# Constant products at the joints, VectorE's chains laid between each other, rank products between key and value groups, in a four-stage transformer kernel

## What is computed

```python
x = x + jnp.tanh(g_xattn[0]) * _L0_xattn_ref(_layernorm(x), ctx, ctx, ...)      # 16 heads, softmax
x = x + jnp.tanh(g_ffn[0]) * _L0_ffn_ref(_layernorm(x), gamma, beta, Wg, ...)   # 8 experts, best 2
x = x + jnp.tanh(g_xattn[1]) * _L1_xattn_ref(_layernorm(x), ctx, ctx, fside, ...)  # with a bias
x = x + jnp.tanh(g_ffn[1]) * _L1_ffn_ref(_layernorm(x), slot_query, ...)        # 16 slots, one expert each
```

## Time and profile before

| | |
|---|---|
| runs | 1320.09, 1323.98, 1328.4 us; median 1323.98 |
| the profiled execution | 1323.91 us, span 1322.1 us, mean granted clock 0.985 |
| TensorE busy | 1268.1 us (96% of the span) |
| VectorE, ScalarE, GpSimd busy | 913.2, 796.0, 747.8 us |
| stages on TensorE | first attention to about 323 us, first expert stage to 775, second attention to about 1110, then the slots |

### The profile page before, as it was taken

How to read it: one execution, slowest core, us unless ns; L and a number is a source line. 1 busy time by engine, 2 the same in 40 slices (tenths; PEclk the granted TensorE clock), 3 DMA queues, 4 the chain that set the end, 5 groups by cost and what they waited for, 6 DMA issues and landing times.

```text
span 1322.1 us, 38089 instructions
## 1 busy us (share of the span) xinstructions
PE 1268.1 (96%) x14700; PEld 1136.9 (86%) x14700; DVE 913.2 (69%) x2362; ACT 796.0 (60%) x1739; POOL 747.8 (57%) x835
## 2 busy tenths in 40 slices
PE   7999999996999999999999988999999999999797
PEld 6888988885999999999999977899999998655476
DVE  4899999995766655566655037999999997321387
ACT  4667777663767777777775435666666655322454
POOL 1478888764577777877875044566666653100231
PEclk8999999998999999999999979999999999999999
DMA  6575555552777777777776610631111110699812
GB/s 214 189 250 200 174 200 194 166 200 66 258 219 222 219 227 238 216 224 217 226 238 241 278 49 26 241 117 50 50 50 50 50 46 22 253 428 426 322 59 71
DMA packets 103890, 237.50 MB, mean 180 GB/s; under 512 B 8992, under 2 KB 86176, under 8 KB 91296
## 3 DMA queue, kind: packets, MB, share of 16 engines
q1 hardware_dynamic: 97568, 218.29, 48.3%
q0 software_dynamic: 6144, 16.79, 3.9%
HBM read 174.22 MB, written 60.82 MB: 178 GB/s over the span
## 4 chain that ended last, share of the span: by engine, by line
PE 88%; DVE 6%; DMA 2%; issue 2%; ACT 1%; SPq 0%; POOL 0%; DVEq 0%; ACTq 0%; PEldq 0%; POOLq 0%
PE ps L2061 14%; PE psT L2046 7%; PE ps L690 6%; PE psS L667 5%; PE ps L1038 5%; PE ps L984 4%; PE psT L676 4%; PE psS L2046 3%; PE ps L2046 3%; PE ps L967 2%; PE ps L1001 2%; PE ps L911 2%; PE psT L682 2%; PE ps L701 2%; DMA arena<-wset_dram 2%
## 5 line engine op out<-in xcount | busy, mean ns | idle before, releaser
L2014 POOL TENSOR_TENSOR wb_lo<-arena,wb_hi 128x2048 fp32r<-128x2048 f32 x64 | 297.8, 4654 | 93.7 <-ACT wb_hi L2134 93.7
L2061 PE MATMUL ps<-wb_hi,hT_hi 128*128 128x256 f32 x528 | 151.6, 287 | 0.8 <-DVE hT_lo L2187 0.8
L676 PE MATMUL psT<-arena 32*128 32x128 f32 x2048 | 151.8, 287 | 0.4 <-ACT arena L1208 0.4
L2061 PE MATMUL ps<-wb_lo,hT_hi 128*128 128x256 f32 x528 | 147.7, 280 | 0.0
L2061 PE MATMUL ps<-wb_hi,hT_lo 128*128 128x256 f32 x528 | 147.6, 280 | 0.0
L667 PE MATMUL psS<-arena 32*128 32x256 f32 x1024 | 143.2, 398 | 0.7 <-ACT arena L1284 0.4
L2134 ACT CAST wb_hi<-arena 128x1024 fp32r<-128x1024 f32 x128 | 130.7, 1045 | 1.4 <-DMA arena<-w_dram 0.9
L676 PEld LDWEIGHTS psT<-arena 32*128 32x128 f32 x2048 | 126.9, 189 | 1.4 <-issue 0.9
L1623 POOL TENSOR_TENSOR arena<-arena,eps_sb 128x1 f32<-128x1 f32 x94 | 23.4, 249 | 156.2 <-DVE arena L1497 106.1
L2199 DVE TENSOR_TENSOR arena<-ps,arena 128x512 f32<-128x512 f32 (+1 forms) x39 | 25.4, 650 | 120.8 <-PE ps L2061 80.4
L1636 POOL DMA_INDIRECT arena<-xs_rows,slot_i x64 | 64.5, 1008 | 70.1 <-DMA xs_rows<-arena 55.1
(11 more groups left out here) (494 smaller groups left out, 3867.1 us busy)
## 6 DMA issues: line engine op xcount, KB each, us to landing
arena<-wset_dram SPq DMA_DIRECT2D x24, 2048.0 KB, 16.9
xs_rows<-arena SPq DMA_DIRECT2D x33, 1024.0 KB, 7.6
arena<-w_dram SPq DMA_DIRECT2D x32, 1028.0 KB, 5.8
arena<-w_dram SPq DMA_DIRECT2D x32, 1024.0 KB, 5.9
arena<-w_dram SPq DMA_DIRECT2D x7, 2052.0 KB, 13.6
w_sb<-xs_rows SPq DMA_DIRECT2D x33, 256.0 KB, 2.7
xs_rows<-arena SPq DMA_DIRECT2D x33, 256.0 KB, 5.5
arena<-ctxT_dram SPq DMA_DIRECT2D x63, 128.0 KB, 4.2
```

Source lines behind the costliest of these rows:

```text
L676: nc.tensor.matmul(psT[:, b, j * P:(j + 1) * P], kbd_[p, (k - 1) % NK, c, par, :], qT[p, (k - 1) % 3, c, :], start=j == 0, stop=False, ski ...
L2014: nc.gpsimd.tensor_tensor(wb_lo[:, u % 2, part], wb_raw[:, u % 2, part], wb_hi[:, u % 2, part], ALU.subtract).then_inc(w_g.sem, 1)
L2061: last = nc.tensor.matmul(ps[5][:, t * D:(t + 1) * D], hp[:, f, t * P:(t + 1) * P], wp[:, f, :], start=f == 0 and t == 0 and n == 0, stop= ...
```

## The change

It has four parts; the arithmetic on the data stays the same.

*The ends of the stages.* The first tables move from `setup` into step -1 of VectorE's loop, those made from columns alone stand in step -1, the rest behind the m chain of step 0 and without the wait for all constants. `keys(0)` goes to bank 2 and waits for its own load only; `values(0)` and the gate sums stand in step -1 behind the turned input; in steps 0 and 1 `values(k+1)` stands behind the second scores. The load of x[2] stands in setup, ahead of the wide output weights. ScalarE's copies of the first keys and values follow.

*Constant products.* Products of constants whose result nobody reads: 10 of 128 columns ahead of `keys(0)`, 14 of 512 columns at the end of the first attention, 5 behind the first `turned(0)` of the first expert stage, 8 ahead of the second attention's loop and 8 in its step 0 ahead of the row maxima.

*VectorE's order in the first attention.* The one-hot stands ahead of the statistics; the moments of tile k+2 between the reciprocal and `att`; the positions ahead of the moments' aggregate; the rows sent and normalised between the products and the sums of the slots; the logits, best values and best experts between the four pieces of the m chain (for the last steps at their old place).

*The ranks.* The two products stand between the two half groups of keys or values (steps 4 to 30); in steps 31 to 33 they stay, and those of tile 31 move from step 35 to step 34, between `ahead_keys(3)` and `ahead_values(3)`.

Counts of the semaphores are renumbered to fit. The diff, cut to its core:

```diff
+        def first_tables(dve):
+            dve.wait_ge(ld_first, 48)
+            nc.vector.tensor_scalar(qcol[:, 0, :], col["bq0"], QSCALE, None, ALU.mult)
+            nc.vector.tensor_tensor(bkm[:, :, :], col["bk0"][:, :, None].to_broadcast([P, C, 2]),
+                                    cv["parity"][:, None, :].to_broadcast([P, C, 2]), ALU.mult).then_inc(setup_v, 1)
+            for c in range(C):
+                last = nc.vector.tensor_scalar(wc[:, c, :], wg_sb[:, c, :], col["gamma"][:, c:c + 1], None, ALU.mult)
+            last.then_inc(fold_v, 1)
...
+            nc.vector.tensor_copy(ident_b[:, :], cv["ident"])
+            for j in range(4):
+                last = nc.vector.tensor_scalar(pick[:, j, :], ones[:, :], cv["pick"][:, j:j + 1], None, ALU.mult)
+            last.then_inc(setup_v, 1)
...
+        def column_tables(dve):
...
         def tables(dve):
-            dve.wait_ge(ld_const, 16 * 5)
...
-                    if A and valid(k + 4) and k + 4 >= 2:
+                    if A and valid(k + 4) and k + 4 >= 3:
...
                         if m:
+                            if i >= 5:
+                                ranks(i - 5)
                             pe.wait_ge(pre_a.sem, pre_a.at(i, "xT"))
...
                         if n_:
+                            ranks(i - 4)
                             pe.wait_ge(pre_a.sem, pre_a.at(i + 1, "xT"))
...
+                def ranks(i):
+                    pe.wait_ge(rk_v.sem, rk_v.at(i, "both"))
+                    before(pe, av_a.sem, av_a.at(i + 2, "av"))
+                    for n_, m in enumerate((before_r[:, :], both_rows[:, :])):
+                        last = nc.tensor.matmul(ps[4][:, n_ * E0:(n_ + 1) * E0], m, both[:, :], start=True, stop=True)
+                    last.then_inc(rk_p.sem, 1)
...
                 if A:
-                    gate_sums(pe)
-                    pe.wait_ge(ld_first, 48)
+                    pe.wait_ge(setup_v, 2)
+                    for _ in range(10):
+                        nc.tensor.matmul(ps[4][:, 0:P], ones[:, :], ones[:, :], start=True, stop=True)
                     pe.wait_ge(ld_kv, 16)
-                    keys(0, 6)
-                    values(0, 7)
+                    keys(0, 2)
                 else:
...
+                    for _ in range(8):
+                        nc.tensor.matmul(ps[4][:, :], ident_b[:, :], ident_b[:, None, :].to_broadcast([P, 4, P]),
+                                         start=True, stop=True)
...
+                    if A and k == -1:
+                        pe.wait_ge(ld_first, 48)
                     if A and valid(k + 1):
                         input_turned(k + 1)
+                    if A and k == -1:
+                        values(0, 7)
+                        gate_sums(pe)
...
-                        if A:
+                        if A and k == 2:
                             pe.wait_ge(pre_a.sem, pre_a.at(k + 1, "xT"))
-                        values(k + 1, 5 if A else 6)
+                        if not A or k == 2:
+                            values(k + 1, 5 if A else 6)
...
-                    if A and valid(k - 4):
-                        pe.wait_ge(rk_v.sem, rk_v.at(k - 4, "both"))
-                        before(pe, av_a.sem, av_a.at(k - 2, "av"))
-                        for n_, m in enumerate((before_r[:, :], both_rows[:, :])):
-                            last = nc.tensor.matmul(ps[4][:, n_ * E0:(n_ + 1) * E0], m, both[:, :], start=True, stop=True)
-                        last.then_inc(rk_p.sem, 1)
+                    if A and B - 2 < k < B + 3:
+                        ranks(k - 4)
...
                     scores(k, 1)
+                    if A and 0 <= k < 2:
+                        pe.wait_ge(pre_a.sem, pre_a.at(k + 1, "xT"))
+                        values(k + 1, 5)
...
+                    if not A and k == 0:
+                        for _ in range(8):
+                            nc.tensor.matmul(ps[4][:, :], ident_b[:, :], ident_b[:, None, :].to_broadcast([P, 4, P]),
+                                             start=True, stop=True)
                     if valid(k):
...
                         ahead_keys(3)
+                        ranks(B - 1)
                         ahead_values(3)
...
+                        pe.wait_ge(stash_a, 1)
+                        for _ in range(14):
+                            nc.tensor.matmul(ps[5][:, :], ident_b[:, :], ident_b[:, None, :].to_broadcast([P, 4, P]),
+                                             start=True, stop=True)
...
+                    if A and k == -1:
+                        act.wait_ge(setup_v, 3)
+                        act.wait_ge(kv_p.sem, key_at(0))
+                        keys(0, 2)
...
+                    if A and k == -1:
+                        act.wait_ge(kv_p.sem, value_at(0))
+                        values(0, 7)
...
+                def next_moments(dve, i):
+                    dve.wait_ge(ld_x[i % 2], dma_at(i, i % 2))
+                    nc.vector.bn_stats(stat[:, 0, :], x_all[:, i + 1]).then_inc(ln_v.sem, 1)
+
+                def logits(i):
+                    dve.wait_ge(out_v.sem, out_v.at(i, "t"))
+                    nc.vector.scalar_tensor_tensor(out=lg, in0=lg_sum, scalar=rq[:, 1:2], in1=bg_sb[:, :],
+                                                   op0=ALU.mult, op1=ALU.add).then_inc(rt_v.sem, 1)
+
+                def best_values(i):
+                    dve.wait_ge(rt_v.sem, rt_v.at(i, "lg"))
+                    nc.vector.max(top_val[:, i, :], lg).then_inc(rt_v.sem, 1)
+
+                def best_experts(i):
+                    dve.wait_ge(rt_v.sem, rt_v.at(i, "top"))
+                    nc.vector.max_index(idx8[:, :], top_val[:, i, :], lg).then_inc(rt_v.sem, 1)
...
+                        first_tables(dve)
...
-                    if A and k == 0:
-                        tables(dve)
...
-                    if A and valid(ln_i):
-                        dve.wait_ge(out_v.sem, out_v.at(ln_i, "x"))
-                        nc.vector.bn_stats(stat[:, 1, :], x_all[:, ln_i + 1]).then_inc(n2_v.sem, 1)
                     if A and valid(sl_i):
                         dve.wait_ge(rt_v.sem, rt_v.at(sl_i, "idx"))
                         nc.vector.tensor_tensor(oh2, idx8[:, 0:2, None].to_broadcast([P, 2, E0]),
                                                 cv["iota8"][:, None, :].to_broadcast([P, 2, E0]), ALU.is_equal)\
                             .then_inc(rk_v.sem, 1)
+                    if A and valid(ln_i):
+                        dve.wait_ge(out_v.sem, out_v.at(ln_i, "x"))
+                        nc.vector.bn_stats(stat[:, 1, :], x_all[:, ln_i + 1]).then_inc(n2_v.sem, 1)
+                    if A and valid(sl_i):
                         dve.wait_ge(rk_v.sem, rk_v.at(sl_i, "oh"))
                         before(dve, rk_p.sem, rk_p.at(sl_i - 1, "rank"))
                         nc.vector.tensor_tensor(both[:, :], oh2[:, 0, :], oh2[:, 1, :], ALU.add).then_inc(rk_v.sem, 1)
...
+                    if A and k == B + 3:
+                        normalised_rows(B - 1)
...
+                    if A and valid(nxt):
+                        next_moments(dve, nxt)
...
-                    if A:
-                        rows_sent(ln_i - 3)
-                    if A and k <= B:
-                        normalised_rows(ln_i)
...
                     if A and valid(sl_i):
                         dve.wait_ge(rk_p.sem, rk_p.at(sl_i, "rank"))
                         nc.vector.tensor_tensor(pos2, ps[4][:, 0:E0], next_row[:, :], ALU.add).then_inc(rk_v.sem, 1)
                         nc.vector.tensor_tensor(next_row[:, :], ps[4][:, E0:2 * E0], next_row[:, :], ALU.add)\
                             .then_inc(rk_v.sem, 1)
+                    if valid(nxt):
+                        dve.wait_ge(ln_v.sem, ln_v.at(nxt, "stats"))
+                        nc.vector.bn_aggr(mv[:, 0, :], stat[:, 0, :]).then_inc(ln_v.sem, 1)
+                    if A and k == -1:
+                        column_tables(dve)
                     if A and valid(sl_i):
                         dve.wait_ge(rk_v.sem, rk_v.at(sl_i, "run"))
                         nc.vector.tensor_tensor(ohp2, oh2, pos2[:, None, :].to_broadcast([P, 2, E0]), ALU.mult)\
                             .then_inc(rk_v.sem, 1)
+                    if A:
+                        rows_sent(ln_i - 3)
+                    if A and k <= B:
+                        normalised_rows(ln_i)
...
                         nc.vector.tensor_copy(m2[:, :, 0, :], mx).then_inc(mx_v.sem, 1)
+                        if A and valid(rt_i):
+                            logits(rt_i)
                         dve.wait_ge(mx_v.sem, mx_v.at(k, "hi"))
                         nc.vector.tensor_tensor(mrest, mx, m2[:, :, 0, :], ALU.subtract).then_inc(mx_v.sem, 1)
+                        if A and valid(rt_i):
+                            best_values(rt_i)
                         dve.wait_ge(mx_v.sem, mx_v.at(k, "rest"))
```

(30 more changed lines are left out.)

52 lines of the change are left out of this document (21 added, 31 removed).

## The result

| | before | after |
|---|---|---|
| median | 1326.10 us (11 runs) | 1312.34 us (11 runs, 1306.65 to 1325.62) |
| ratio | | 0.9911, 95% interval 0.9885 to 0.9937 |
| the profiled execution | 1323.91 us, span 1322.1, clock 0.985 | 1309.47 us, span 1307.7, clock 0.999 |

The ratio is -11.8 us, with its interval -8.3 to -15.2; the two profiled executions are 14.4 us apart. The forecast was 1308 with 1302 to 1318 as its range: right in sign and in most places; in size the median came out 4 us short. One place was not in the prediction at all, and it decides part of the spread of the changed kernel. One execution of the repetition x10, 1327.85 us, is more than 1.5% above the shortest of its kernel and is left out of its ratio.

What follows compares the result with a forecast made beforehand. PE was taken to bound the long stages, leaving gains at joints: start -6.4, VectorE's order 0, ranks +0.3, first attention's end -5.5, second attention's start -4.0; -15.6 from 1323.91 gives 1308.3 us, range 1302 to 1318.

Steps and rivals of the forecast that it cites:

- What bounds the kernel: Long middle stages: PE is the bound, so faster other engines cannot shorten the first attention's step; time is lost at joints.
- the ranks' move: First attention, two rank products moved into the middle of the group: -1 to +2.4 us over 27 steps, taken +0.3.
- Whatever a joint gives is handed on whole: All joints: gains pass on in full because the stages behind are PE-bound; the sum is made joint by joint.
- rival 5: Joints: the next wait, an expert weight's split or scatter's landing, takes the gains; each keeps a quarter, 1320 us; chance 0.04.
- The start: Kernel start: earlier keys and scores, shorter waits for m, and an avoided clock fall give -6.4 us, ends -2.5 and -7.5.
- rival 1: Early first attention: the clock falls again, start gives only -3.5, in all -12.7 us, 1311; chance 0.24.
- VectorE's order: First attention, some 28 steps: reordered instructions gain 0 because PE never waits for VectorE; ends 0 and +8.7 us.
- The end of the first attention: Joint to the first expert stage: earlier last scatter and full clock give -5.5 us together, ends -1.5 and -6.
- The second attention's start: Second attention's first steps: constant products keep the clock up, -4.0 us, ends -1.5 and -6.
- VectorE as the bound: First attention: VectorE, not PE, sets the step, so 8 to 13 us more come off, about 1297; chance 0.05.
- the late m chain: First attention, m of every step: the chain comes late and PE stalls, 1317 to 1330 us; chance 0.06.
- Further falls of the clock (1 and 2): Early first attention (1311 us, chance 0.24), or a later joint, first expert stage or second attention (about 1313, chance 0.15).

Runs made afterwards that it cites:

- x10: The unmodified changed kernel measured once more, beside others on the same chip: 1317.17 us, ratio 0.9911.
- x8: The changed kernel without the ten constant products at the very start: 1315.95 us, ratio 0.9894.
- x1: The changed kernel without any of its constant products, the rest of the change kept: 1319.92 us, ratio 0.9953.
- x6: The changed kernel with VectorE's plan of the six single units moved to the first expert stage's very start: 1308.40 us, ratio 0.9849.
- x7: x6 with the constant products of the second attention's start spread over its gaps (two, two, four, six): 1309.79 us, ratio 0.9842.
- x11: Repetition of x6, the changed kernel with the early plan of the single units: 1309.65 us, ratio 0.9864.
- x5: The changed kernel without the eight constant products ahead of the second attention's first row maxima: 1318.07 us, ratio 0.9915.
- x3: The kernel before with only VectorE's new order in the first attention and the ranks between the half groups: 1325.14 us, ratio 0.9978.
- x2: The kernel before with the constant products alone, at the same places: 1325.74 us, ratio 0.9990.
- x4: The kernel before with only the last tile's ranks moved, to between its keys and values made ahead: 1324.38 us, ratio 0.9989.
- x9: The kernel before with only VectorE's plan of the single units moved to the first expert stage's start: 1323.14 us, ratio 0.9957.

## Why the prediction was right, step by step

- *What bounds the kernel* held: no wait of PE in the first attention's middle, 8.80 us a step before and after, and, but for one stop of 1.3 us (see the ranks' move), all of the difference at joints. "Whatever a joint gives is handed on whole" did not hold in one place, the third unit of the first expert stage: of 4.9 us gained from m(31) to the second turn 1.95 were taken back in this execution, and 5.3 more in x8's. This is rival 5 in a form that was not in it: the text named a weight's split as what PE waits for, and it was GpSimd's split of the weights that held VectorE's plan. The kernel before shows its smaller form, 0.8 us, in the stretch that was read as bound by PE (432.16 of 433.00 us).
- *The start*: -6.4 forecast, -8.2 measured to m(3). Keys at 5.54 (5.1 forecast): they wait for the first context and not for their weights, since without the ten products they begin at 5.43 and 5.55 (x1, x8), released by that load. So the ten cost nothing there, as said, but their price was wrong: 4.37 us instead of 2.6, as each is listed as two products. First scores -4.7 against -2.4, outside its end of -3.5: mis-sized was the clock, up at 5.3 us instead of "a microsecond or two earlier" than 12.7, so queries and values ran at full clock too. The waits for m did not vanish as said (-1.1): PE then waited 0.46 and 0.76 us for ScalarE's copy of the queries. The fall from 22.9 to 29.8 us was avoided here and in x6, x7 and x11, which start alike. In x5 the clock fell from 18.6 to 25.4 us and m(3) came 3.4 us later than here, and in x10 it fell at 54.8; so rival 1 happened in part of the executions, and that the profiled one kept its clock is luck.
- *VectorE's order*: 0, measured 0 (x3). The m chain, whose serial end was priced +8.7, came no later than the product with m needed it.
- *The ranks' move*: +0.3; from m(4) to m(31) the change is -0.15 us over 27 steps. The other 1.3 us of that stretch is one stop of PE inside a group, with no semaphore behind it:

```profile
50.50 0.27 PE L695 MATMUL psT<-mT,pick 32*128 32x128 bf16 x3
51.95 0.32 PE L695 MATMUL psT<-mT,pick 32*128 32x128 bf16 x5 [1.18 <-issue]
```

  Stops in the same group, of 1.1 to 1.4 us, are in the profiles of x5, x7, x10 and x11 too, and shorter ones of about 0.3 us in x6 and x2. All seven kernels have the ten products at the start; the six without them (before, x1, x3, x4, x8, x9) have no such stop. That PE comes to this place earlier is not what separates them: in x5 it comes at 53.9 us and stops, in x1 at 53.5 and in x8 at 54.0 and does not. A load of instructions, 16 KB on a DMA queue of its own, begins 0.1 to 1.9 us ahead of the place in all thirteen profiles, so this alone is no reason either. The cause stays open; if the ten bring the stop, they give back 1 to 1.5 of the 3 us that they gain up to m(3).

- *The end of the first attention*: the scatter -2.9 (-2.6 forecast), of which the rows' load lost 0.7, since it came 2.5 us after the last scatter's end instead of 1.7; clock and turn -2.75 (-2.9 forecast). -4.9 in all against -5.5.
- *The second attention's start*: -3.5 against -4.0, in x10 -1.9; from the first turn to step 2 19.42 us, where 18.8 were forecast. That the second eight run while VectorE's chain is still going holds at full clock (x6); here the clock fell for 3.4 us.
- *Rivals.* VectorE as the bound and the late m chain fell (x3). Further falls of the clock (1 and 2) came in part of the executions; with the held instructions they are what the runs offer for a median of -11.8 where the forecast said -15.6: x6, which has none held there, has a ratio of 0.9849, 20 us under the kernel before.
- *The size.* -11.8 us lies nearer to rivals 1 and 2 (-12.7, and -11 to -13) than to the forecast, whose own range of 1304 to 1312 the median just misses. Being more than 1% faster was given 0.53 and being within 1% 0.44; it was 0.9%. Errors also offset each other in the profiled execution: the start gave 1.8 us more than its term, and the middle and the third unit, priced at 0.3 and at nothing, took 1.2 and 1.95.

## What to carry to other kernels

Look first for the stretches that run at half clock and for what PE waits for ahead of them: filling a wait at a joint with constant products was worth some 3 us there, as long as they end inside the wait; at half clock they can stick out. At the start the same products brought nothing with the old order around them, in the one profile of it. A chain on an engine that the bound never waits for can be shortened by an eighth and bring nothing. Where a gain is made ahead of a stage, look at the small waits inside that stage: 0.8 us before was the mark of a collision that grew to 6 in some profiles.

## What the runs showed of the hardware

Small instructions of VectorE, reading and writing SBUF, were held while GpSimd worked on two tensors of 128x2048: 4.15 to 4.63 us instead of 0.15 to 0.22. Not all that ran beside it were: in x5 two reductions with one SBUF input, begun 0.08 and 0.31 us behind GpSimd's start, took 0.20 us each, and the instruction after them 4.15. VectorE's instructions with an input in PSUM went on beside the same instructions at their usual 0.69 us. The Trainium skill (GPSIMD Engine Reference, Specifications) says that GpSimd's SBUF interfaces are shared with VectorE, with "contention with DVE instructions in a 2-port perf mode or with two SBUF inputs"; the trace agrees for the 128x8 ones, which have two SBUF inputs. The 1x6 one of x8 and two on 128x6 (x2, x5) have a single input tensor, and whether they ran in such a mode no run shows. In every case the wait lasted to the end of GpSimd's instruction.

PE's clock is not a matter of the program alone: in one execution of the changed kernel it fell at 773.3 us only, in another (x10) at 54.8, 300.5, 775.0 and 1304.1 us, and its executions reach from 1306.65 to 1325.62 us. A single profile of this kernel is therefore no measure of what one joint costs; the stretches that repeat over several kernels are.
